# A step's norm and maximum moved from VectorE to GpSimd in a recurrent scan, and its hardware loops written out

## The reference, cut to what matters

```python
def step(h, inp):                       # h: 4 x 256 x 16, one step a token
    dAt, dBt, xt, Ct = inp
    h = dAt * h + dBt * xt[..., None]
    h_norm = jnp.sqrt(jnp.sum(h * h, axis=(1, 2), keepdims=True))
    scale = jnp.minimum(20.0 / (h_norm + 1e-08), 1.0)
    h = h * scale
    y = jnp.einsum('bdn,bn->bd', h, Ct) + Dp * xt
    return (h, y)
_, ys = jax.lax.scan(step, h0, (dA_t, dB_t, x_t, C_t))
```

## Time and profile before

| what | value |
|---|---|
| time, median of 3 runs | 1827.41 us (1826.48 to 1827.98) |
| profiled execution, its own time | 1828.65 us |
| profiled execution, span | 1826.9 us |
| VectorE busy | 1657.4 us, 91% of the span |
| TensorE busy (matmul) | 1396.5 us, 76% |
| ScalarE busy | 1082.4 us, 59% |
| GpSimd busy | 932.5 us, 51% |
| instructions on VectorE / GpSimd | 11513 / 1403 |

### The profile page before, as it was taken

The page is one execution under the profiler, slowest core; times in us unless marked ns, Lnnn a source line. Parts: engine busy times, 40 slices in busy tenths (PEclk is TensorE's granted clock), DMA queues, the critical chain, the costliest instruction groups (busy, mean ns, idle before and its releaser), DMA issues.

```text
span 1826.9 us, 38640 instructions
## 1 busy us (share of the span) xinstructions
PE 1396.5 (76%) x8889; PEld 1271.0 (70%) x8889; DVE 1657.4 (91%) x11513; ACT 1082.4 (59%) x2502; POOL 932.5 (51%) x1403
## 2 busy tenths in 40 slices
PE   6788979597968787697868786888859795879820
PEld 4577878496858687686758685877758685768720
DVE  7587999999998999999999999899999999899967
ACT  5775666556556654666565656566465655566424
POOL 5365555455555555455545554554555555555534
PEclk9858989898989899898989898898989898999965
DMA  9443011101020102100020102000110102010076
GB/s 334 149 202 95 20 32 45 51 19 35 19 76 23 30 19 65 31 23 29 21 74 24 30 24 71 22 25 27 41 51 22 35 19 74 21 31 22 18 247 223
DMA packets 97034, 110.47 MB, mean 60 GB/s; under 512 B 25680, under 2 KB 84176, under 8 KB 95632
## 3 DMA queue, kind: packets, MB, share of 16 engines
q1 hardware_dynamic: 87504, 86.26, 14.5%
q0 software_dynamic: 7776, 21.24, 3.7%
q10 hardware_dynamic: 1504, 0.22, 0.1%
HBM read 62.22 MB, written 45.48 MB: 59 GB/s over the span
## 4 chain that ended last, share of the span: by engine, by line
issue 38%; POOL 30%; DVE 22%; PE 6%; DMA 2%; POOLq 1%; ACT 1%; SPq 0%; DVEq 0%; ACTq 0%
POOL arena L567 22%; DVE arena L819 4%; DVE arena L790 3%; POOL moe L545 3%; POOL xrow L539 3%; DVE arena L804 3%; DVE arena L796 3%; DVE arena L811 3%; PE ps L1056 2%; DVE arena L815 1%; DVE arena L836 1%; DVE arena L793 1%; POOL arena L573 1%; DVE arena L808 1%; PE ps L1095 1%
## 5 line engine op out<-in xcount | busy, mean ns | idle before, releaser
L567 POOL TENSOR_TENSOR arena<-arena,neghalf 128x1 f32<-128x1 f32 x1025 | 605.3, 591 | 728.8 <-DVE arena L793 722.9
L815 DVE SCALAR_TENSOR_TENSOR arena<-arena 128x128 f32<-128x128 f32 x1024 | 360.5, 352 | 69.3 <-POOL arena L567 69.3
L1164 PE MATMUL ps<-ident,arena 128*128 128x128 f32 x1024 | 199.4, 319 | 228.8 <-ACT arena L908 190.1
L1164 PEld LDWEIGHTS ps<-ident,arena 128*128 128x128 f32 x1024 | 177.6, 245 | 252.7 <-issue 250.4
L983 ACT ACTIVATE arena<-ps,arena 128x128 f32<-128x128 f32 x1024 | 292.7, 373 | 53.7 <-PE ps L1168 52.8
L790 DVE TENSOR_TENSOR arena<-arena 128x128 f32<-128x128 f32 x1024 | 295.1, 288 | 23.6 <-issue 18.8
L1180 PE MATMUL ps<-arena,wf 128*128 128x256 f32 x1280 | 305.9, 387 | 10.9 <-ACT arena L995 10.9
L796 DVE CUSTOM_DVE_ANT_0 arena<-arena 128x128 f32<-128x128 f32 x1024 | 306.9, 300 | 0.0
L1168 PE MATMUL ps<-arena,pick 128*128 128x128 f32 x2048 | 286.6, 285 | 15.6 <-ACT arena L983 14.3
L804 DVE CUSTOM_DVE_ANT_0 arena<-arena 128x128 f32<-128x128 f32 x1024 | 292.6, 286 | 1.8 <-PE ps L1145 1.8
L1194 PE MATMUL ps<-wp,arena 128*128 128x256 f32 x1280 | 289.5, 379 | 0.0
(11 more groups left out here) (155 smaller groups left out, 1517.8 us busy)
## 6 DMA issues: line engine op xcount, KB each, us to landing
feed<-arena SPq DMA_DIRECT2D x9, 1024.0 KB, 3.9
arena<-feed SPq DMA_DIRECT2D x34, 256.0 KB
arena<-in_x SPq DMA_DIRECT2D x16, 512.0 KB, 6.4
moe<-zeros SPq DMA_DIRECT2D x8, 1024.0 KB, 9.5
wf<-in_c_fc SPq DMA_DIRECT2D x8, 1024.0 KB, 5.0
wp<-in_c_proj SPq DMA_DIRECT2D x8, 1024.0 KB, 6.0
arena<-moe SPq DMA_DIRECT2D x12, 512.0 KB, 8.6
arena<-dx SPq DMA_DIRECT2D x66, 64.0 KB
```

Of the source, the lines that this page charges most:

```text
L567: g.tensor_tensor(sv[:, slot, 1:2], mx, neghalf[:, 0:1], ALU.pow).then_inc(s_ready, 1)
L815: v.scalar_tensor_tensor(hr[:, slot, :], vv, sv[:, before, 1:2], ur[:, slot, :], ALU.mult, ALU.add)\
L1164: last = t.transpose(ps[q % 2][:, j * P:(j + 1) * P], tanhb[:, f, :, s], ident[:, :])
```

## The change

- On VectorE the maximum (L793), the reciprocal (L808) and the multiply-and-sum (L819) go. The factor 1/400 moves into the two reductions. sums gets a second buffer, used by turns.
- On GpSimd a step's scale is now four instructions, each behind a wait for the one before: ta = sums0 * s + sums1, qv = ta * s + norm of the input, mx = max(qv, 1), sv = mx ** -0.5. This is Horner's form of s^2 sums0 + s sums1 + norm, with s the scale of the step before, from the same engine. The first waits for s_ready and T_ready, at the first step of a block for be_stage too.
- GpSimd's steps have the same place against gathers, scatters and windows; the call at the very first step is left out.
- ScalarE's copy to ring_be waits for s_ready in place of q_ready.
- The hardware loops of all five engines become 8 turns of the Python loop, VectorE's one of 1024 steps: straight code with constants in waits and addresses.

```diff
@@ -116,9 +117,9 @@
         dxt = take(P)
         vv = take(P)
         junk = take(2 * P).rearrange("p (f d) -> p f d", f=2)
-        junkq = take(2)
         ac = take(2)
-        sums = take(2)
+        sums = take(2 * 2).rearrange("p (f w) -> p f w", f=2)
+        ta = take(1)
         qv = take(1)
         mx = take(1)
         sv = take(RING * 2).rearrange("p (t w) -> p t w", w=2)
@@ -400,23 +402,23 @@
...
-            with sp.Fori(0, CH) as m:
-                load_dx(m * BPB, bass.ds(m * P, BLK))
+            for m in range(CH):
+                load_dx(m * BPB, span(m * P, BLK))
                 sp.wait_ge(mm1_ps, m * (TPE * FC // 2) + 1)
-                sp.dma_start(wf, c_fc[bass.ds(m, 1), :, :].rearrange("e (k p) f -> p (e k) f", p=P)).then_inc(wf_in, 16)
+                sp.dma_start(wf, c_fc[span(m, 1), :, :].rearrange("e (k p) f -> p (e k) f", p=P)).then_inc(wf_in, 16)
                 sp.wait_ge(mm2_ps, m * (TPE * 2) + 1)
-                sp.dma_start(wp, c_proj[bass.ds(m, 1), :, :].rearrange("e (k p) d -> p (e k) d", p=P)).then_inc(wp_in, 16)
...
@@ -553,7 +555,7 @@
             pool.sem_inc(win_ready, 1)
-            pool.sem_inc(s_ready, BLK)
+            pool.sem_inc(s_ready, BLK + 1)
@@ -561,9 +563,19 @@
             gather(0, slot_src[:, 0:1])
             gather(1, slot_src[:, 1:2])
-            def scale_of(slot, count):
-
-                pool.wait_ge(m_ready, count)
+            def scale_of(step):
+
+                slot, last = step % RING, sv[:, (step - 1) % RING, 1:2]
+                if step % BLK == 0:
+                    pool.wait_ge(be_stage, step // BLK + 1)
+                pool.wait_ge(s_ready, step + 1 + BLK)
+                pool.wait_ge(T_ready, step + 1)
+                g.tensor_scalar(ta, sums[:, step % 2, 0:1], last, sums[:, step % 2, 1:2], ALU.mult, ALU.add).then_inc(h1_ready, 1)
+                pool.wait_ge(h1_ready, step + 1)
+                g.tensor_scalar(qv, ta, last, ring_be[:, slot, 1:2], ALU.mult, ALU.add).then_inc(q_ready, 1)
+                pool.wait_ge(q_ready, step + 1)
+                g.tensor_scalar(mx, qv, 1.0, None, ALU.max).then_inc(m_ready, 1)
+                pool.wait_ge(m_ready, step + 1)
                 g.tensor_tensor(sv[:, slot, 1:2], mx, neghalf[:, 0:1], ALU.pow).then_inc(s_ready, 1)
             def windows(half, ccols, count, blk):
@@ -590,14 +602,15 @@
...
-                    scale_of((k - 1) % RING, m * P + (k + 1 + BLK))
+                    if m * P + k > 0:
+                        scale_of(m * P + k - 1)
                     if k % BLK == 0:
-                        windows(1 - k // BLK % 2, ccol[:, bass.ds(m * P + k, BLK)], m * P + (k + 1 + BLK), m * BPB + (k // BLK + 1))
+                        windows(1 - k // BLK % 2, ccol[:, span(m * P + k, BLK)], m * P + (k + 1 + BLK), m * BPB + (k // BLK + 1))
                     if k == 1:
...
@@ -775,51 +788,34 @@
-            for s_, c_ in ((T_ready, BLK), (v_ready, BLK), (ac_ready, BLK), (m_ready, BLK), (h_ready, BLK), (q_ready, BLK)):
-                dve.sem_inc(s_, c_)
+            dve.sem_inc(h_ready, BLK)
             v.memset(hr, 0.0).then_inc(h_ready, 1)
-            v.memset(qv, 1.0).then_inc(q_ready, 1)
-            dve.wait_ge(s_ready, BLK)
             dve.wait_ge(u_done, 2)
-            with dve.Fori(0, CH) as m:
-                for k in range(P):
-                    slot, before = k % RING, (k - 1) % RING
-                    now = m * P + (k + 1 + BLK)
-
-                    dve.wait_ge(h_ready, now)
-                    v.tensor_tensor(vv, hr[:, before, :], da[:, slot, :], ALU.mult).then_inc(v_ready, 1)
-
-                    dve.wait_ge(q_ready, now)
-                    v.tensor_scalar(mx, qv, 1.0, None, ALU.max).then_inc(m_ready, 1)
-
-                    dve.wait_ge(v_ready, now)
-                    v.tensor_tensor_reduce(out=junk[:, 0, :], in0=vv, in1=ur[:, slot, :], scale=2.0, scalar=0.0,
-                                           op0=ALU.mult, op1=ALU.add, accum_out=ac[:, 1:2])
-                    if k % QUAD == QUAD - 1:
-
-                        dve.wait_ge(u_done, m * (P // QUAD) + (k // QUAD + 3))
-                    elif k % BLK == 0:
-
-                        dve.wait_ge(y_done, m * BPB + (k // BLK + 2))
-                    v.tensor_tensor_reduce(out=junk[:, 1, :], in0=vv, in1=vv, scale=1.0, scalar=0.0,
-                                           op0=ALU.mult, op1=ALU.add, accum_out=ac[:, 0:1]).then_inc(ac_ready, 1)
-
-                    dve.wait_ge(m_ready, now)
-                    v.reciprocal(sv[:, before, 0:1], mx)
-
-                    dve.wait_ge(ac_ready, now)
-                    v.tensor_reduce(out=sums, in_=ac.unsqueeze(2).broadcast_to([P, 2, 32]), axis=AX.X, op=ALU.add,
-                                    apply_transpose=True).then_inc(T_ready, 1)
-
-                    dve.wait_ge(s_ready, now)
-                    v.scalar_tensor_tensor(hr[:, slot, :], vv, sv[:, before, 1:2], ur[:, slot, :], ALU.mult, ALU.add)\
-                        .then_inc(h_ready, 1)
-
-                    dve.wait_ge(T_ready, now)
-                    v.tensor_tensor_reduce(out=junkq, in0=sums, in1=sv[:, before, :], scale=1.0 / CLAMP ** 2, scalar=ring_be[:, slot, 1:2],
-                                           op0=ALU.mult, op1=ALU.add, accum_out=qv).then_inc(q_ready, 1)
-            dve.wait_ge(q_ready, NT + 1 + BLK)
-            v.tensor_scalar(mx, qv, 1.0, None, ALU.max).then_inc(m_ready, 1)
+            for step in range(NT):
+                slot, before = step % RING, (step - 1) % RING
+
+                dve.wait_ge(h_ready, step + 1 + BLK)
+                v.tensor_tensor(vv, hr[:, before, :], da[:, slot, :], ALU.mult).then_inc(v_ready, 1)
+
+                dve.wait_ge(v_ready, step + 1)
+                v.tensor_tensor_reduce(out=junk[:, 0, :], in0=vv, in1=ur[:, slot, :], scale=2.0 / CLAMP ** 2, scalar=0.0,
+                                       op0=ALU.mult, op1=ALU.add, accum_out=ac[:, 1:2])
+                if step % QUAD == QUAD - 1:
+
+                    dve.wait_ge(u_done, step // QUAD + 3)
+                elif step % BLK == 0:
+
+                    dve.wait_ge(y_done, step // BLK + 2)
+                v.tensor_tensor_reduce(out=junk[:, 1, :], in0=vv, in1=vv, scale=1.0 / CLAMP ** 2, scalar=0.0,
+                                       op0=ALU.mult, op1=ALU.add, accum_out=ac[:, 0:1]).then_inc(ac_ready, 1)
+
+                dve.wait_ge(ac_ready, step + 1)
+                v.tensor_reduce(out=sums[:, step % 2, :], in_=ac.unsqueeze(2).broadcast_to([P, 2, 32]), axis=AX.X, op=ALU.add,
+                                apply_transpose=True).then_inc(T_ready, 1)
+
+                dve.wait_ge(s_ready, step + 1 + BLK)
+                v.scalar_tensor_tensor(hr[:, slot, :], vv, sv[:, before, 1:2], ur[:, slot, :], ALU.mult, ALU.add)\
+                    .then_inc(h_ready, 1)
             def last_product(i):
                 f = i % 2
@@ -960,12 +956,12 @@
...
-            with act.Fori(0, CH) as m:
+            for m in range(CH):
                 for g in range(BPB):
                     half, f = g % 2, g // 4
-                    act.wait_ge(q_ready, m * P + (g * BLK + 1))
-                    a.activation(ring_be[:, half * BLK:(half + 1) * BLK, :], be[:, bass.ds(m * P + g * BLK, BLK), :],
+                    act.wait_ge(s_ready, m * P + (g * BLK + 1))
+                    a.activation(ring_be[:, half * BLK:(half + 1) * BLK, :], be[:, span(m * P + g * BLK, BLK), :],
```

More of the change, by code:

```diff
@@ L54, in build @@
     ctx = ExitStack()
+    span = lambda first, count: slice(first, first + count)
     with ctx:
@@ L268, in build @@
         h_ready = sem("h_ready")
+        h1_ready = sem("h1_ready")
         q_ready = sem("q_ready")
@@ L401, in store_y @@
                 sp.dma_start(ys[at, :, :].rearrange("t b (k d) -> (t b k) d", k=DH), ysb).then_inc(y_out, 16)
[L403 to L404 removed]
+            for m in range(CH):
+                load_dx(m * BPB, span(m * P, BLK))
                 sp.wait_ge(mm1_ps, m * (TPE * FC // 2) + 1)
[L407 removed]
+                sp.dma_start(wf, c_fc[span(m, 1), :, :].rearrange("e (k p) f -> p (e k) f", p=P)).then_inc(wf_in, 16)
                 sp.wait_ge(mm2_ps, m * (TPE * 2) + 1)
[L409 removed]
+                sp.dma_start(wp, c_proj[span(m, 1), :, :].rearrange("e (k p) d -> p (e k) d", p=P)).then_inc(wp_in, 16)
                 for g in range(BPB):
@@ L415, in _ @@
                         sp.wait_ge(tanh_done, m * 2 + f + 1)
-                        load_feed(1 - f, bass.ds(m + f, 1))
+                        load_feed(1 - f, span(m + f, 1))
                     if g > 0:
-                        load_dx(m * BPB + g, bass.ds(m * P + g * BLK, BLK))
-                    store_y(m * BPB + g, bass.ds(m * P + g * BLK, BLK))
+                        load_dx(m * BPB + g, span(m * P + g * BLK, BLK))
+                    store_y(m * BPB + g, span(m * P + g * BLK, BLK))
             load_dx(NBLK, slice(NBLK * BLK, (NBLK + 1) * BLK))
```

(6 more changed lines are left out.)

4 lines of the change are left out of this document (2 added, 2 removed).

## The result

The changed kernel takes 2589.31 us (median of 3 runs, 2587.88 to 2590.74), the kernel before 1827.41: 1.417 times as long, with a 95% interval of 1.415 to 1.420. All of it is in the scan.

What follows compares the result with a forecast made beforehand. The prediction took VectorE's step as today's bound and a GpSimd ring of 2.02 us as the new one: 1024 steps, 2068 us, plus 247 make a 2315 us loop, +704 on 1827.4, say 2530 us; range 2170 to 2880.

Steps and rivals of the forecast that it cites:

- ring: GpSimd's four chained instructions from one step's scale to the next, with their waits: 2.02 us a step, the bound; chance 0.88.
- beside the ring, in all: Other work in GpSimd's queue, paid in full: windows 53 us, gathers and scatters 192, row copies 2; together 247 us.
- The multiply-adds: GpSimd's two tensor-scalar operations with column scalars: 0.291 us each, taken from L573 as nearest in size.
- the range's upper end: Dearest prices on GpSimd, 0.408 us for two operations and 0.291 for the maximum: step 2.36 us, time 2878, range to 2880.
- The waits: GpSimd waiting for its own last result, four times a step at 0.165 us: 0.66 us.
- Rival 3: GpSimd's operations also held until VectorE's two-input instructions end: about 0.5 us more a step, time 3044 us; chance 0.07.
- The sign that I gave: Evidence for GpSimd being held by VectorE: small operations over 0.4 us, with starts lining up with ends of VectorE's two-input instructions.
- Rival 2: GpSimd's chain stays hidden behind VectorE and the kernel is not slower: some 1799 us; chance 0.02.
- Rival 4: GpSimd's small operations far below 0.14 us or waits near half those seen: step 1.3 to 1.6 us, time about 1949; chance 0.03.
- VectorE's part: Three instructions removed from VectorE stood in latency that stays: at most 0.03 us a step saved, cycle 1.44 us.
- Gathers and windows: On GpSimd, each gather or scatter adds about 1.2 us (160 of them), each window update 0.82 us (64).
- The turn-rounds: VectorE's hardware-loop turn-round, seven times, 18.8 us in all: removed by writing out, but counted as no gain or loss.

Runs made afterwards that it cites:

- a7: The changed kernel with the maximum left out on GpSimd, the power taking the norm itself: 2260.64 us, 1.237 of the kernel before.
- a5: The changed kernel with constants in place of the column scalars in GpSimd's two multiply-adds: 2241.25 us, 1.226 of the kernel before.
- a4: The changed kernel without VectorE's two reductions and with its product and state update narrowed to one column: 2375.77 us, 1.300 of the kernel before.
- b1: The kernel before with only the hardware loops of all five engines written out as Python loops: 1822.08 us, 0.998 of the kernel before.
- b7: The kernel before with four engines' hardware loops written out and GpSimd's kept: 1809.64 us, 0.990 of the kernel before.
- b9: The kernel before, all loops written out, with the maximum alone moved from VectorE to GpSimd: 1927.85 us, 1.055 of the kernel before.
- b4: The kernel before, all loops written out, with each gather and scatter of 128 rows as two of 64: 1871.9 us, 1.027 of the kernel before.

## Why the prediction was right

The forecast was 2530 us, the time is 2589, and the mechanism is the one forecast: a ring of four dependent instructions on GpSimd (a7), with VectorE waiting at each state update and every window, gather and scatter adding to the time. But two terms of the ring were wrong by 0.3 us each, in opposite directions. That the forecast came within 59 us is the luck of this cancelling; the path, the bound and the direction are not.

| term of a step, us | forecast | measured in the profile after |
|---|---|---|
| two multiply-adds with column scalars | 0.582 | 0.455 + 0.432 = 0.887 |
| maximum | 0.188 | 0.221 |
| power | 0.591 | 0.568 |
| four waits for its own result | 0.66 | (100.9 + 101.6 + 89.5 + 85.5) / 1024 = 0.369 |
| ring | 2.02 | 2.045 |
| beside the ring, in all | 247 | 2373 - 1024 x 2.045 = 279 |

The measured durations and waits are means over all steps, also those behind a gather, where the multiply-adds are short; an undisturbed step takes 2.10 us, and from it 2373 - 1024 x 2.10 = 223 us are left for the rest.

**The multiply-adds** were sized by L573, a tensor-tensor operation of 16 columns. What it had not in it: the column scalars (a5: 0.34 us a step for both) and a stronger slowing by VectorE (a4: 0.20 us for both). The two figures overlap: together they are more than the 0.305 us that were missing. I had no row with column scalars to see their price by. The upper bound, 0.408 for each, was passed as well; with the waits as forecast the ring would have been 2.336 us, just under the 2.36 of the range's upper end.

**The waits** were taken from the earlier trace rows, which stand in a hardware loop, each with a register instruction in front that carries the wait. The changed kernel has no loop there, and b1 and b7 show that this halves the first of them. The diff said it: waits on registers become waits on constants, and I costed the writing-out only as turn-rounds.

**Rival 3** (VectorE's reads hold GpSimd up), chance 0.07, is a real part of the time: 213 us by a4, not the 512 it was priced at. Its mechanism fits the rows better than its chance says. L573 starts at 999.93, 0.07 us into L817, which ends at 1000.21, and ends at 1000.42; one step later it starts 0.13 us into L817, which ends at 1002.31, lasts 0.43 and ends at 1002.52. Both end 0.21 us behind L817, wherever they start; some 60 that meet the product L798 instead, 0.29 us into it, last 0.38 us and end 0.21 us behind its end. On VectorE the small product in b1 and the reduction in the earlier trace rows end a fixed time behind GpSimd's pass too. Ends tied to the other's end are what being held until then looks like. What was wrong is the price: I added the whole rest of VectorE's instruction, but of the first multiply-add's 0.34 us some 0.13 (my estimate, 0.34 - 0.21) runs off while it is held. It loses 0.15 us a step and the second, beside the first reduction, 0.11, not 0.5 together. The sign that I gave, starts that line up with VectorE's ends, was the wrong one to look for; it is the ends. The Trainium skill, "SBUF — State Buffer", section "SBUF: two separate sides", has the pair of ports as a lock for the whole instruction, taken by whichever starts first. The ends agree with a hold until the other's end. Two things don't show it: the power lasts 0.59 us beside VectorE and 0.57 without, and in b1 the small product, by the records 0.01 us the earlier to start, is the one held.

**Rival 2** (hidden, not slower) is out: the ring was 2.05 us against its 1.03. **Rival 4** counted on waits near half of the seen ones, and they were; but the operations were not cheap.

**VectorE's part** came out as told, in the distances that can be seen while it waits for GpSimd. From product to first reduction it takes 0.35 us without the maximum (0.33 with it), from second reduction to transposed sum 0.32 (0.33), from state update to product 0.38 (0.41). Three instructions left and at most 0.03 us in a hole came back; b9 shows the same for the maximum alone, in steps of 1.48 us that no ring lengthens.

**Gathers and windows** came out a little under their price. From power to power the steps with a gather take 3.23 us and those with a scatter 3.15, against 2.10: 1.13 and 1.05, where 1.2 was put. The queue itself is held for about 1.24 us, but the two multiply-adds behind it meet no two-input instruction of VectorE and last 0.34 each. Steps with a window update take 2.68 us: 0.57, where 0.82 was put with the long waits.

**The changed profile** was foretold with GpSimd busy for some 70% and idle 0.16 us at a time; it is 82% and 0.08 to 0.10 us, the same two mis-sized terms seen from the other side.

**The turn-rounds** (18.8 us) were said to be hidden by the ring; that holds, and b1 shows that even in the old kernel about half of them were eaten by a collision (60 steps longer by 0.28 us, less the 0.12 us that the window cost before, are some 10 us).

## What to carry to other kernels

In a recurrence with two engines, add up the ring that each engine closes with its own results, waits included; short instructions that stand in another's latency cost nothing where they are, and their full length plus a wait once moved into a ring on the other engine. Before taking a price from a trace, look whether the row has the same kind of operand as the new instruction will have, and whether its wait stands on the operation or on an instruction in front. Where two engines slow each other, compare the ends of the instructions as well as their durations. An edit that shortens a wait off the path can shift a transfer or a pass into a worse collision, so look at the steps that became longer, and try keeping the loop of that one engine. That last point was seen in this kernel alone.

## What the runs showed that I had not expected

- GpSimd's wait for its own result takes 0.08 to 0.11 us where it stands on the operation, and 0.16 to 0.17 us where a register or semaphore instruction in front carries it (b1 against b7, and 136 steps of the changed kernel).
- The first multiply-add, where it starts under a two-input instruction of VectorE, ends 0.21 us behind that instruction's end, however late it started; with constants (a5) it is 0.05 us.
- A tensor-scalar operation of one column on GpSimd lasts 0.34 us with two column scalars and no two-input instruction of VectorE beside it, mostly 0.38 to 0.50 with one; with constants 0.19 to 0.22 and 0.23 to 0.35.
- An indirect gather of 64 rows takes 1.09 us, one of 128 rows 1.17 (b4).
- The kernel with the slower waits is the faster one: with GpSimd's loop kept and the rest written out it takes 1809.64 us, 1.0% less than before and 0.7% less than with GpSimd's loop written out too.
